# First convolution part of an attention hybrid in 64x64 quarters, and logits of two row blocks side by side

## What is computed

```python
x = x + conv_part(group_norm(x))     # t2 = conv 1x3 (w2, 64x64 channels), t7 = depthwise 1x5 of t2,
                                     # t8 = depthwise 5x5 of x, dilated by 2, t10 = correlation part of t2
                                     # result: t8 - (t10 - t7)
t = tokens(x)                        # 3136 tokens of 64 channels
t = t + linear_attention(layer_norm(t))     # 16 heads, elu features, cos/sin position weights
u = layer_norm(t)
logits = einsum('bsd,ed->bse', u, gate_w) + gate_b      # 32 experts
probs = softmax(logits, axis=tokens); vals, idx = top_k(probs, 8)
t = t + scatter(expert_ffn(gather(u, idx)) , vals)
```

## Times and profile before

| | |
|---|---|
| median of 3 runs | 3843.64 us (3842.21 to 3851.14) |
| profiled execution, its own time | 3844.39 us |
| its span in the trace | 3842.6 us |
| PE busy | 3480.2 us (91%) |
| PE weight loads | 1723.1 us (45%) |
| DVE busy | 2928.1 us (76%) |
| ACT busy | 1710.6 us (45%) |
| POOL busy | 1777.5 us (46%) |
| mean granted TensorE clock | 0.964 of full speed |

### The profile page before, as it was taken

How to read it: one execution, slowest core, us unless ns; L and a number is a source line. 1 busy time by engine, 2 the same in 40 slices (tenths; PEclk the granted TensorE clock), 3 DMA queues, 4 the chain that set the end, 5 groups by cost and what they waited for, 6 DMA issues and landing times.

```text
span 3842.6 us, 52421 instructions
## 1 busy us (share of the span) xinstructions
PE 3480.2 (91%) x17588; PEld 1723.1 (45%) x17588; DVE 2928.1 (76%) x3293; ACT 1710.6 (45%) x1808; POOL 1777.5 (46%) x1638
## 2 busy tenths in 40 slices
PE   3799998999999998999989999999989999999976
PEld 2444444444543445444544445434444445444453
DVE  6887877878688877878778786888778786758823
ACT  0166524754256533665246542565336552443210
POOL 1067721866148741677228761487317771211200
PEclk8899999999999999999999999999999999999967
DMA  1000000000000001000000000000010000100045
GB/s 50 18 1 1 1 17 27 1 1 1 22 23 1 1 1 44 1 1 1 18 27 1 1 1 26 18 1 1 1 44 1 1 1 18 31 1 1 1 123 212
DMA packets 18670, 70.92 MB, mean 18 GB/s; under 512 B 8781, under 2 KB 13421, under 8 KB 13485
## 3 DMA queue, kind: packets, MB, share of 16 engines
q1 hardware_dynamic: 18365, 67.10, 5.6%
HBM read 37.26 MB, written 29.84 MB: 17 GB/s over the span
## 4 chain that ended last, share of the span: by engine, by line
PE 48%; issue 21%; POOL 15%; DVE 11%; ACT 3%; DMA 1%; SPq 1%; POOLq 0%; DVEq 0%; ACTq 0%
PE ps_D L1554 16%; POOL arena L570 9%; POOL UA L580 4%; PE ps_E L1518 4%; PE ps_C L1543 4%; PE ps_B L1501 4%; PE ps_A L1501 3%; PE ps_D L1325 2%; DVE arena L939 2%; PE ps_E L1529 2%; PE ps_B L1305 2%; PE ps_A L1305 1%; PE ps_C L1472 1%; PE ps_E L1567 1%; DVE ST L986 1%
## 5 line engine op out<-in xcount | busy, mean ns | idle before, releaser
L570 POOL TENSOR_TENSOR arena<-arena,UHL 128x896 f32<-128x896 f32 x525 | 1087.6, 2089 | 168.0 <-ACT UHL L722 149.2
L1554 PE MATMUL ps_D<-region,small 128*128 128x448 f32 x1792 | 768.3, 552 | 22.8 <-DVE OS L1149 22.6
L1122 DVE TENSOR_TENSOR region<-region,ps_C 128x896 f32<-128x896 f32 x448 | 485.9, 1085 | 279.8 <-PE ps_C L1543 279.2
L722 ACT ACTIVATE UHL<-arena,W8C 128x896 f32<-128x896 f32 x525 | 541.9, 1032 | 0.0
L1554 PEld LDWEIGHTS ps_D<-region,small 128*128 128x128 f32 x1792 | 316.9, 191 | 324.1 <-issue 285.3
L758 ACT ACTIVATE EQ<-ps_B,NEG 128x896 f32<-128x896 f32 x224 | 225.7, 1008 | 476.2 <-PE ps_B L1501 476.2
L580 POOL TENSOR_TENSOR UA<-region,CS 128x128 f32<-128x128 f32 (+1 forms) x400 | 229.3, 575 | 408.1 <-PE ps_C L1472 358.9
L1472 PE MATMUL ps_C<-region,UA 128*128 128x512 f32 (+1 forms) x800 | 378.4, 595 | 2.9 <-ACT region L656 2.8
L758 ACT ACTIVATE EQ<-ps_A,NEG 128x896 f32<-128x896 f32 x224 | 225.5, 1007 | 339.4 <-PE ps_A L1501 339.4
L939 DVE SCALAR_TENSOR_TENSOR arena<-arena,W8C 128x448 f32<-128x448 f32 (+1 forms) x243 | 364.9, 1523 | 0.0
L1089 DVE SCALAR_TENSOR_TENSOR region<-region,ps_A 128x1024 f32<-128x1024 f32 (+1 forms) x200 | 242.2, 1211 | 100.0 <-ACT region L740 98.2
(11 more groups left out here) (299 smaller groups left out, 5824.1 us busy)
## 6 DMA issues: line engine op xcount, KB each, us to landing
arena<-x SPq DMA_DIRECT2D x8, 1568.0 KB, 7.1
t_keep<-Y SPq DMA_DIRECT2D x7, 1568.0 KB, 7.2
w_keep<-region SPq DMA_DIRECT2D x7, 784.0 KB, 5.6
CST<-t_keep SPq DMA_DIRECT2D x2, 1568.0 KB, 9.8
small<-t_keep SPq DMA_DIRECT2D x2, 1568.0 KB, 12.3
plane<-w_keep SPq DMA_DIRECT2D x4, 784.0 KB, 16.1
UHL<-t_keep SPq DMA_DIRECT2D x2, 1568.0 KB, 12.6
out<-CST SPq DMA_DIRECT2D x2, 1568.0 KB, 12.1
```

The costliest lines, as they stand in the source:

```text
L570: pool.tensor_tensor(out=X[:, cut], in0=X[:, cut], in1=PRODUCT[m % 3], op=ALU.add).then_inc(pool_taps.sem, 1)
L722: act.activation(PRODUCT[m % 3].rearrange("p (h w) -> p h w", w=W), g_window(2 * g * ROWS + 2 * (k // 5), 2 * (k % 5) - 4, 2 * ROWS), ACT. ...
L1122: dve.tensor_tensor(out=q, in0=q, op=ALU.mult, in1=here.area(key)[:, :].rearrange("p (c n) -> p c n", c=2)[:, :, 0:PIX])\
L1554: ins = pe.matmul(here.area(key)[:, 0:PIX], MW[i][:, c, :], Q[s % 3][:, c, :], start=c == 0, stop=c == NCHUNK - 1)
```

## The change

`front` works in the same quarters as `conv`: four groups instead of seven chunks, in slots 57, 59, 61 and 63, twelve matmuls of 64x64 each (448 columns, in the last group 224), and ACT empties each group with four copies of 64 partitions. In the logits two blocks n and n+1 share a use of an area: the even one goes to output partitions 0 to 63, the odd one to 64 to 127. DVE's waits follow the new names.

```diff
-FRONT_SLOTS = {SLOTS + 1 + n: n for n in range(NPIX)}
+FRONT_SLOTS = {SLOTS + s: g for g, s in enumerate((1, 3, 5, 7))}
...
-                uses += [(("t2", FRONT_SLOTS[j]), "AB"[j % 2])] if j in FRONT_SLOTS and not last else []
+                uses += [(("t2", FRONT_SLOTS[j]), "AB"[FRONT_SLOTS[j] % 2])] if j in FRONT_SLOTS and not last else []
...
-            uses += [(("lg", n), misc()) for n in range(NPIX)]
+            uses += [(("lg", g), misc()) for g in range(NG)]
...
-            def front(here, chunks):
+            def front(here, groups):
 
-                for n in chunks:
-                    key = ("t2", n)
+                for g in groups:
+                    key, (parts, rows) = ("t2", g), CONV_PARTS[g]
                     act.wait_ge(*here.filled(key))
-                    act.activation(T2[:, 3 + n * ROWS:3 + (n + 1) * ROWS, 2:2 + W],
-                                   here.area(key)[:, 0:PIX].rearrange("p (h w) -> p h w", w=W),
-                                   ACT.Copy).then_inc(*here.empty(key))
+                    for b, row in enumerate(parts):
+                        for i in range(2):
+                            src = here.area(key)[HALVES[i ^ b], i * 512:i * 512 + rows * W]
+                            ins = act.activation(T2[HALVES[i], 3 + row:3 + row + rows, 2:2 + W],
+                                                 src.rearrange("p (h w) -> p h w", w=W), ACT.Copy)
+                    ins.then_inc(*here.empty(key))
...
-                for n in range(NPIX):
-                    key = ("lg", n)
+                for g in range(NG):
+                    key = ("lg", g)
                     act.wait_ge(*here.filled(key))
-                    act.activation(LG[:, n * PIX:(n + 1) * PIX], here.area(key)[0:C, 0:PIX], ACT.Identity,
-                                   bias=GBC[:, 0:1]).then_inc(*here.empty(key))
+                    for n in range(2 * g, min(2 * g + 2, NPIX)):
+                        ins = act.activation(LG[:, n * PIX:(n + 1) * PIX], here.area(key)[HALVES[n % 2], 0:PIX],
+                                             ACT.Identity, bias=GBC[:, 0:1])
+                    ins.then_inc(*here.empty(key))
...
                         if k == 0:
-                            for at in here.all_emptied([("t2", n) for n in range(2 * g, min(2 * g + 2, NPIX))]):
-                                dve.wait_ge(*at)
+                            dve.wait_ge(*here.emptied(("t2", g)))
...
-            def front(here, pair, chunks):
+            def front(here, pair, groups):
 
-                for n in chunks:
-                    if n == 0:
+                for g in groups:
+                    if g == 0:
                         pe.wait_ge(*g_ready.at(pair, 1))
-                    key = ("t2", n)
+                    key, (parts, rows) = ("t2", g), CONV_PARTS[g]
                     pe.wait_ge(*here.room(key))
+                    passed(pe)
                     for k in range(3):
-                        ins = pe.matmul(here.area(key)[:, 0:PIX], W2T[:, k, :],
-                                        g_window(4 + n * ROWS, k - 1, ROWS), start=k == 0, stop=k == 2)
+                        for b, row in enumerate(parts):
+                            for i in range(2):
+                                ins = pe.matmul(here.area(key)[HALVES[i ^ b], i * 512:i * 512 + rows * W],
+                                                W2T[HALVES[i], k, HALVES[i]],
+                                                g_window(4 + row, k - 1, rows)[HALVES[i]],
+                                                start=k == 0, stop=k == 2)
                     ins.then_inc(*here.fill(key))
...
-                for n in range(NPIX):
-                    key = ("lg", n)
+                for g in range(NG):
+                    key = ("lg", g)
                     pe.wait_ge(*here.room(key))
-                    pe.matmul(here.area(key)[0:C, 0:PIX], GWT[:, :], U2[:, n * PIX:(n + 1) * PIX],
-                              start=True, stop=True).then_inc(*here.fill(key))
+                    for n in range(2 * g, min(2 * g + 2, NPIX)):
+                        ins = pe.matmul(here.area(key)[HALVES[n % 2], 0:PIX], GWT[:, :],
+                                        U2[:, n * PIX:(n + 1) * PIX], start=True, stop=True)
+                    ins.then_inc(*here.fill(key))
```

More of the change, by code:

```diff
@@ L221, in front_uses @@
         def front_uses(first=0):
-            return [(("t2", n), misc()) for n in range(first, NPIX)]
+            return [(("t2", g), misc()) for g in range(first, NG)]
         def correlation_uses():
@@ L488, in _ @@
             last_load(1)
-            for w in Here("last").all_emptied([("lg", n) for n in range(NPIX)]):
+            for w in Here("last").all_emptied([("lg", g) for g in range(NG)]):
                 sp.wait_ge(*w)
@@ L786, in _ @@
             act.wait_ge(*zeroed.first(2))
-            front(start, range(NPIX))
+            front(start, range(NG))
             columns(start)
@@ L1022, in routing @@
             def routing(here):
-                for w in here.all_emptied([("lg", n) for n in range(NPIX)]):
+                for w in here.all_emptied([("lg", g) for g in range(NG)]):
                     dve.wait_ge(*w)
@@ L1360, in conv @@
                     passed(pe)
-                    for w in here.all_emptied([("t2", m) for m in range(NPIX)]):
+                    for w in here.all_emptied([("t2", m) for m in range(NG)]):
                         pe.wait_ge(*w)
@@ L1640, in _ @@
             group_norm(start, 0, "gvar")
-            front(start, 0, range(NPIX))
+            front(start, 0, range(NG))
             correlations(start)
```

## The result

| | before | changed |
|---|---|---|
| median, same chip | 3847.39 us (4 runs, 3842.21 to 3853.42) | 3812.55 us (4 runs, 3810.20 to 3813.80) |
| ratio | | 0.9912, 95% interval 0.9894 to 0.9930 |
| profiled execution, span | 3844.39, 3842.6 | 3812.63, 3810.8 |

What follows compares the result with a forecast made beforehand. TensorE was taken to bound the first convolution part, with VectorE next, and TensorE to set the logits' pace. Savings of 35.0 and 12.8 us, together 47.8, off 3844.4 gave 3797 us, range 3783 to 3813.

Steps and rivals of the forecast that it cites:

- the larger term: First convolution part in quarters: VectorE becomes the bound, `out_parts` of slot 65 starts 5.0 us earlier; seven pairs, 35.0 us.
- the prediction's own sign: Whole pair: the prediction calls itself wrong if the pair shortens by less than 5 or more than 8 us.
- The other two signs of being wrong: First convolution part: wrong if a group takes over 3 us, or if taps wait for copies.
- The price of quarters and the edges: First part on TensorE: 16.1 us of chunks become 8.2, plus 1.0 for edges (0.25 each group), saving 6.9 us per pair.
- rival 2: First part: each entry into quarters costs the full uncovered load, 1.0 us per group; 37 us saved, 3807 us; chance 0.14.
- Slots 57 to 59: Start of first part: slot 58 loses 2.49 us, two edges add 0.25 each; scaling of slot 60 starts 2.0 us earlier.
- Slots 60 to 65: VectorE's own 14.93 us becomes the bound over TensorE's 13.2; TensorE idles some 1.6 us before the broadcast of slot 63.
- Copies in the first part: ScalarE's four copies per group, 2.1 to 2.5 us, stay hidden, with 1 us to spare in the tightest case.
- The logits: Logits before `routing`: ScalarE binds with copies 0.51 us apart; 1.5 us in each of seven pairs, 2.3 last, 12.8 us.
- Both hang on slot 65, so both shift together: Behind slot 65: the TensorE chain from fold to correlations and VectorE's remaining taps shift together, keeping the 5.0 us saving.
- The rival of the clock: Behind slot 65: thinner TensorE work halves the clock until the logits, 13.5 us more per pair, 3939 us; chance 0.03.
- VectorE's wait for the correlations still about 2.8 us: End of VectorE's remaining taps: they end 2.76 us before the correlations, and this wait was to stay about 2.8 us.

Runs made afterwards that it cites:

- the two kernels with the bound back on TensorE: Changed kernel with VectorE copying logits of groups 1 and 3, and two or one tap pieces brought forward into slot 59: 3787.75 and 3787.96 us.
- the snake: Changed kernel with the two logits copies of every second group in the other order, so some neighbours read the same half: 3809.94 us, one run.
- the halves: Kernel before with only the first convolution part in quarters, 3818.55 us (0.9926), and kernel before with only the logits changed, 3837.04 us (0.9975).
- first part only: Kernel before with only the first convolution part in quarters, logits as before: 3818.55 us, ratio 0.9926.
- copies shared: Changed kernel with VectorE copying the logits of groups 1 and 3, ScalarE those of 0 and 2: 3799.10 us, ratio 0.9879.
- filled kernel: Changed kernel with two extra matmuls, result never read, in slot 66 before the fold: 3810.05 us, ratio 0.9903.
- the three with the old first part: Kernel before (3847.39 us), the same with ScalarE's first logits copy held until the third matmul (3851.83, one run), and with only the logits changed (3837.04).
- the ten with quarters: Changed kernel, its first convolution part alone, and eight edits of the changed kernel (copy order, filling, taps forward, copies shared, combinations): 3787.75 to 3818.55 us.

## Why the prediction was partly right

The sign, the range (3783 to 3813, at its very edge) and the mechanism of the larger term hold; the number is 15.5 us too low. By the prediction's own sign it is wrong: the pair was to shorten by 5 to 8 us. From `out_parts` of slot 65 in one pair to that in the next it shortens by 4.2 us (445.6 to 441.5, mean of six), and the four stages of the table give 4.6 us per pair. The other two signs of being wrong stayed away: a group takes 2.45 us and no tap waits for a copy. Two steps failed: the overlap of the logits' copies, and the steps behind slot 65, which were to shift and not to grow. By the steps:

- **The price of quarters and the edges.** Six passes of a group take the time of the earlier trace rows, and the edge was assumed at 0.25 us. Slot 57 takes 0.36 us longer than before, from 3.98 (528.42 to the broadcast at 532.40) to 4.34 (526.48 to 530.82), so the pair of edges costs 0.36 us: 0.09 going in, 0.16 at the end and 0.11 in the first output product behind it. This is nearer to the 0.25 than to rival 2's 1.0. TensorE's saving, put at 6.9 us per pair, is 32.69 - 26.08 = 6.6 us, as the two kernels with the bound back on TensorE show.
- **Slots 57 to 59.** The scaling of slot 60 comes 13.21 us after the stage's start instead of 14.79: 1.58 us earlier, not 2.0. The edges take 0.72 instead of 0.5, and slot 58 loses 2.30 us and not 2.49 (broadcast to broadcast 2.98 after 5.28), since part of the chunk's 2.49 was the step from the fold into full matmuls, which the output product now takes.
- **Slots 60 to 65.** VectorE takes 14.33 us where 14.93 was forecast. An instruction that finds its input ready starts some 0.1 us before the one ahead ends: 547.10 against 546.03 + 1.15. The waits of before had hidden that, and taking only the waits away left it out. Five such starts make some 0.4 of the 0.6 us; the rest are VectorE's waits for its own results, 0.68 us before and 0.51 now. TensorE waits 0.60 us ahead of the broadcast of slot 63, where 1.6 stood, and 1.38 ahead of the fold, a wait that the prediction left out. The two slips cancel: drain 5.15 us per pair against 5.0, 36.0 against 35.0 us.
- **Copies in the first part.** Hidden, as said. A group takes ScalarE 2.20 us, and no tap waits for it.
- **The logits, failed term.** "Back to back they overlap: 0.91 long, 0.80 from start to start, so 0.51 here, and at worst 0.63." They are 0.65 us apart. The row was of copies over all partitions, one after the other; the change makes each copy read the other half, and the snake shows that this is what costs the overlap. The seven copies need 3.90 us from first to last instead of 3.06, and with the first one 0.13 us later the step gains 0.50 us per pair where 1.5 stood: 7 us missing. `routing` starts 6.0 us after the first product, not 5. The last pair gave 2.7 against 2.3, but 1.2 of that came with the clock, as the halves show; at an equal clock it is 1.4.
- **"Both hang on slot 65, so both shift together", failed.** The steps behind the drain became longer by 7.4 us. 1.9 of it are in all seven pairs, 0.09 us in O-C, where TensorE waits 0.97 instead of 0.88 us between the fold and the tokens, and 0.18 in C-T; why is open. The other 5.5 us are in the four pairs with a drop, 0.42 in O-C and 0.97 in C-T each. The rival of the clock had the place right and the size wrong: not 13.5 us per pair but 1.4, in four pairs of seven. "The thinnest 10 us there will still be some 8 busy" was right by its number (3.62 + 4.40 of 10), and the clock dropped all the same. Those kernels whose TensorE waits 1.38 us before the fold with nothing to fill it (changed, first part only, copies shared, snake) have drops in 4, 2, 1 and 3 of seven pairs, 10 of 28. Those where it is filled or shorter have none in 42, nor have the three with the old first part in 21. The filled kernel's seven pairs alone could be chance (about 1 in 20 at the rate of 10 in 28), the 42 together can't. That the thin stretch is what lets the clock drop is thereby shown. In all ten the clock falls 2.1 to 2.3 us after the start of `out_parts` of slot 65. Which pairs it strikes is open: the same work precedes it in those with and without a drop.
- **"VectorE's wait for the correlations still about 2.8 us".** Now, over the span, at L952, against the earlier trace rows:

```profile
  PE ps_D L1334: 24.9, 7
```

  3.6 us each: what lies between became longer on TensorE's side. Only idle time, without price.
- The K stage took 3.8 us more, the Q stage 2.3 less, the end 1.9 more. These sums move by a few microseconds from kernel to kernel (over all of them K 1021.7 to 1027.9 us, Q 1379.6 to 1386.1), with the places where short stretches at the lower clock fall. The K stage isn't mere scatter, though the change holds no instruction of it: it takes 1021.7 to 1024.1 us in the three kernels with the old first part and 1025.6 to 1027.9 in the ten with quarters. In the changed kernel the lower clock holds for 39.7 us of it, in the kernel before for 33.5. The prediction had nothing there; how the quarters bring it about is open.

Of the 16 us between forecast and profile (47.8 - 31.8), 7.0 are the copies, 7.4 the steps behind the drain, 3.1 the stages that hold nothing of the change (3.8 of them lost in the K stage), and the better drain and last pair give 1.4 back.

## What to carry to other kernels

When an engine's work is cut and another becomes the bound, the forecast must also ask for what the waiting leaves behind: thinner TensorE work at the end of the stage can cost some clock in the next. A pace taken from neighbours in the trace holds for neighbours on the same partitions; a change that makes copies alternate between halves takes away their overlap. And work moved into another engine's idle time must be held against whoever uses the same memory ports beside it: here one tap moved was enough, a second changed nothing, and a third cost 0.65 us per pair.

## What the runs showed of the hardware

- ScalarE's copies of 64x448 from PSUM: 0.52 to 0.54 us apart when both read the same half of the partitions, 0.63 to 0.65 when the half changes. The four copies of a group in the first part, which change the half that they read or the one that they write at each step, take 2.20 us, 0.55 to 0.56 apart at a length of 0.54, and don't overlap either, not even the middle two, which read the same half and write different ones. Whether the written half costs the overlap there or the form of these copies is not shown: no run has them with both halves unchanged.
- GpSimd beside VectorE: conversions of 32x224 from 0.36 to 1.01 and 0.37 to 1.15 us, an addition from 0.60 to 1.34. The roots (L551) show it in the changed kernel too, in seven of 64: those that begin while a tap runs (here the second tap of the row at 552.37, until 554.11). VectorE being busy is not enough: in the kernel before a root begins at 210.96 us beside an operation that reads PSUM, VectorE is busy through all of it, and it takes 2.58 us. Timelines, GpSimd, before and then after:

```profile
558.37 2.58 POOL L551 TENSOR_TENSOR ST<-ST,NEGH 128x14 f32<-128x14 f32 x1
```

```profile
553.19 3.35 POOL L551 TENSOR_TENSOR ST<-ST,NEGH 128x14 f32<-128x14 f32 x1
```

- The granted clock fell after a stretch with TensorE busy 3.6 of 5 us in 10 of 28 pairs, and in none of 63 where it was busy 4.28 or more of the 5 us at the same place.
